# Two-layer cross-attention and FFN on one core: an own buffer for raw weight tiles, batch 0's projection and norm moved into the last two units of attention 0, and W1 loaded step by step

## The reference

```
layer 0:  q   = qdq(norm(x)) @ qdq(wq).T + bq          # qdq: int8 codes with a scale per row
          k,v = context @ wkv.T + bkv                  # 16 heads of 32
          o   = softmax(q k / sqrt(32)) v
          x   = x + qdq(o) @ qdq(wp).T + bp
          h   = layernorm(x) @ W1.T                    # W1 is 2048 x 512
          x   = x + gelu(round(h / 0.1) * 0.1) @ W2.T
layer 1:  cross-attention with a mask, output projection, norm, small FFN with experts
```

## Time and profile before

| | |
|---|---|
| median of 3 runs | 2798.19 us (2797.98 to 2801.25) |
| profiled execution | 2802.59 us, its span 2800.8 us |
| PE busy | 2595.8 us (93%), mean granted clock 0.974 |
| DVE busy | 1809.8 us (65%) |
| ACT busy | 1247.3 us (45%) |
| POOL busy | 1209.9 us (43%) |
| DMA | 400.61 MB, 143 GB/s over the span |

### The profile page before, as it was taken

One profiled execution on the slowest core, in us unless ns is written; L12 is line 12 of the kernel. 1 busy time (PEld: TensorE's weight loads), 2 busy tenths in 40 slices (PEclk: granted clock), 3 DMA queues, 4 the chain that ended last, 5 costly groups with the idle time before them and its releaser, 6 DMA issues. The chain is left out here.

```text
span 2800.8 us, 35487 instructions
## 1 busy us (share of the span) xinstructions
PE 2595.8 (93%) x14024; PEld 1676.8 (60%) x14024; DVE 1809.8 (65%) x2539; ACT 1247.3 (45%) x1873; POOL 1209.9 (43%) x302
## 2 busy tenths in 40 slices
PE   8999899998999999999967998998899999998898
PEld 7888788886444454444425777776343334334676
DVE  4553544556666676766615666554799999996664
ACT  3221212312656656565642222222687878773211
POOL 1000000002999999999950000000577777774110
PEclk9999999999999999999987999999999999998899
DMA  8576666565353534435017434435877777762100
GB/s 296 202 251 217 228 234 239 195 195 140 78 110 62 120 67 99 89 78 109 17 55 261 143 134 165 141 125 132 203 155 156 156 156 156 156 183 98 60 31 31
DMA packets 214856, 400.61 MB, mean 143 GB/s; under 512 B 16697, under 2 KB 92505, under 8 KB 214625
## 3 DMA queue, kind: packets, MB, share of 16 engines
q1 hardware_dynamic: 214688, 398.34, 51.1%
HBM read 256.31 MB, written 140.33 MB: 142 GB/s over the span
## 5 line engine op out<-in xcount | busy, mean ns | idle before, releaser
L1176 POOL TENSOR_TENSOR pooled<-pooled,probs 128x2048 f32<-128x2048 f32 x140 | 640.5, 4575 | 20.1
L1085 ACT ACTIVATE probs<-psum 128x512 f32<-128x512 f32 (+1 forms) x832 | 459.3, 598 | 354.7 <-PE psum L1011 351.7
L1112 DVE TENSOR_REDUCE win_max<-psum 128x1 f32<-128x802 f32 x480 | 453.9, 988 | 168.9 <-PE psum L976 168.7
L1886 DVE TENSOR_SCALAR probs<-psum,bound 128x1024 f32<-128x1024 f32 (+1 forms) x416 | 507.5, 1278 | 43.8 <-PE psum L1782 43.8
L1841 ACT ACTIVATE probs<-probs 128x1024 f32<-128x1024 f32 (+1 forms) x416 | 440.6, 1059 | 112.7 <-DVE probs L1886 74.9
L1917 POOL TENSOR_TENSOR pooled<-pooled,probs 128x2048 f32<-128x2048 f32 x80 | 368.4, 4605 | 79.9 <-ACT probs L1841 79.9
L1011 PE MATMUL psum<-q_st,k_st 128*128 128x512 f32 (+1 forms) x832 | 336.0, 438 | 37.1 <-ACT den_sb L1097 17.9
L1011 PEld LDWEIGHTS psum<-q_st,k_st 128*128 128x128 f32 (+1 forms) x832 | 148.9, 185 | 260.0 <-ACT probs L1085 176.3
L197 POOL TENSOR_TENSOR r_q<-ve_q,minus_half 128x4 f32<-128x4 f32 x8 | 8.7, 1087 | 681.7 <-DVE ve_q L173 681.7
L976 PE MATMUL psum<-k_st,q_st 96*128 96x402 f32 x960 | 266.3, 359 | 6.1 <-DVE o_sb L1143 5.0
L1782 PE MATMUL psum<-q_st,k_st 128*128 128x512 f32 (+1 forms) x832 | 250.8, 423 | 10.2 <-PEq L138 10.2
(11 more groups left out here) (242 smaller groups left out, 4461.8 us busy)
## 6 DMA issues: line engine op xcount, KB each, us to landing
k_st<-k_hi SPq DMA_DIRECT2D x64, 801.0 KB, 11.9
k_st<-k_lo SPq DMA_DIRECT2D x48, 801.0 KB, 11.5
k_hi<-kt_hi SPq DMA_DIRECT2D x32, 801.0 KB, 4.1
k_lo<-kt_lo SPq DMA_DIRECT2D x32, 801.0 KB, 6.2
v_rows<-v_out SPq DMA_DIRECT2D x96, 256.0 KB
v_st<-v_rows SPq DMA_DIRECT2D x24, 768.0 KB
q_st<-q_hi SPq DMA_DIRECT2D x64, 256.0 KB, 10.3
w<-w_hi_d SPq DMA_DIRECT2D x64, 256.0 KB, 3.0
```

Of the source, the lines that this page charges most:

```text
L1085: A.activation(probs[i % NPROBS][0:rows, j, :], bank(score_banks.where["score", u, t, j])[0:rows, :], ACT.Exp, scale=1.0 / ROOT).then_inc( ...
L1112: V.tensor_reduce(win_max[:, r, j, c:c + 1], window(windows.where["max", u, i])[:, :, 0:MV], AX.XY, ALU.max).then_inc(max_done, 1)
L1176: G.tensor_tensor(pooled[u % 2][:], before[:], probs[tile(u, k) % NPROBS][:], ALU.add).then_inc(pool_added, 1)
L1886: V.tensor_scalar(probs[i % NPROBS][0:rows, half * W:half * W + W, :], window(("score", u, t, half))[0:rows], bound[0:rows, u // NG, t:t + 1],
```

## The change

Three things are changed.

1. In the first stage h_raw has a place of its own. SP loads the next raw tile right behind the stores of the last job, in the same tick, without the wait for h_stored. The jobs start at tick 18 and not 12. Layer 0's eight tiles pass through v_out and h_raw, layer 1's through full and step_row two at a time with all low halves on DVE; on ACT and DVE layer 1's tiles come later, from tick 8 on. v_out has three buffers, not four.
2. The projection and norm of batch 0 move from the start of the FFN stage into attention_0. Their tiles (class FirstRows) lie in the place of slot 1, which is free after unit 13. SP loads them at the start of unit 14. DVE quantises behind the spread at tile 11 of unit 14. PE turns the codes at tile 0 of unit 15 (DVE copies them, not ACT) and multiplies at tile 2, through the PSUM windows of the maxima; DVE adds the rows at tile 2 and normalises at tile 4, and POOL takes the root ahead of its last add.
3. W1's chunks 0 to 4 are loaded at the start of the FFN stage, each later one in the step NW2 to FT - 2 of batch 0, behind the W2 chunk of that step. x of batch 1, wq and the mask are loaded in steps 5, 9, 10 and 12, and the waits for wq's semaphore move to where it is used.

The diff's core, in this order: SP's jobs, the two sets of weight tiles and SP's turns for layer 1's; in attention_0 the transposes on PE and their place, DVE's places, and POOL's root; in the FFN stage SP's loads of W1.

```
                 def halves():
-                    for j in range(len(weights.stage), len(weights.tiles)):
-                        weights.on_sp(j)
-                        yield
-                    for _ in range(FIRST_JOB - len(weights.tiles) + len(weights.stage)):
-                        yield
-                    for n, (src, hi, lo) in enumerate(halved):
-                        if n:
-                            Y.wait_ge(h_stored, 32 * n)
+                    for _ in range(FIRST_JOB):
+                        yield
+                    weights[0].wait_staged(Y)
+                    for n, (src, _, _) in enumerate(halved):
                         load(h_raw[:], src, h_landed)
-                        for _ in range(JOB_TICKS - 1):
+                        for _ in range(JOB_TICKS if n else JOB_TICKS - 1):
                             yield
                         Y.wait_ge(h_lo_done, n + 1)
-                        for dst, part in ((hi, h_hi), (lo, h_lo)):
+                        for dst, part in zip(halved[n][1:], (h_hi, h_lo)):
                             store(dst, four(part[:]) if len(dst.shape) == 3 else part[:], h_stored)
-                        yield
...
+            weights = [SplitWeights(sem, v_out + [h_raw], "wa"), SplitWeights(sem, [full, step_row], "wb", pool=False)]
...
+                    def weights_1():
+                        for _ in range(4):
+                            yield
+                        for j in range(2 * KT):
+                            if j == 2:
+                                for _ in range(7):
+                                    yield
+                            if j >= 2:
+                                yield
+                                yield
+                            weights[1].on_sp(j)
...
+                    def first_codes():
+                        for half in range(2):
+                            slot, free = windows.take(("codes", half))
+                            M.wait_ge(*free)
+                            if half == 0:
+                                M.wait_ge(o_coded, 1)
+                            for w in range(2):
+                                m = transposes(window(slot)[:, w, :], first.cols, 2 * half + w)
+                            m.then_inc(q_ps, 1)
+                            windows.freed_by(q_turned, half + 1)
...
+                            if now == (UNITS - 1, 0):
+                                first_codes()
+                            if now == (UNITS - 1, 2):
+                                first_projection()
...
+                        if now == (UNITS - 2, TURN_AT):
+                            V.wait_ge(o_landed, 16)
+                            for _ in quantise_on_dve(own, first.cols, first.step, first.recip, o_coded):
+                                pass
+                        if now == (UNITS - 1, 0):
+                            first_codes()
+                        if now == (UNITS - 1, 2):
+                            first_rows()
+                        if now == (UNITS - 1, CLOSE_AT):
+                            V.wait_ge(y_done, RT)
+                            for _ in norm_on_dve(own, nm, first.rows, first.cols, 0, normed):
+                                pass
...
+                            if u == UNITS - 1 and k == pooled_tiles(u) - 2:
+                                root_on_pool(nm, 0)
...
-                    for f in range(FT):
+                    for f in range(NW2 + 1):
                         load_w1(f)
                         if f < NW2:
                             load_w2(f)
...
+                        if NW2 <= i < FT - 1:
+                            load_w1(i + 1)
+                        if i == 5:
+                            load_x(1)
```

More of the change, by code:

```diff
@@ L65, in f32, with together @@
     return ap.bitcast(F32)
+def together(*sides):
+    while sides:
+        sides = [side for side in sides if next(side, sides) is None]
+        yield
 def three(l_hi, l_lo, r_hi, r_lo):
@@ L749, in pool_program @@
                 def pool_program():
-                    for j in range(len(weights.tiles)):
-                        weights.on_pool(j)
+                    for j in range(2 * KT):
+                        weights[0].on_pool(j)
                     for b in range(B):
@@ L835, in sp_program @@
                     load(rows[:], a["wq0"].rearrange("(r p) d -> p r d", p=P), rows_landed)
-                    for j in range(KT, len(weights.stage)):
-                        weights.on_sp(j)
-                    beside = halves()
+                    for j in range(KT, 2 * KT):
+                        weights[0].on_sp(j)
+                    beside = together(weights_1(), halves())
                     for b in range(B):
@@ L1369, in second_half @@
                             m.then_inc(f_read, 1)
-                    for _ in projected(0):
-                        pass
                     operand(0)
@@ L2288, in out_projection_and_ffn_1 @@
                 close()
+        handover = ExitStack()
+        with ExitStack() as brief:
+            first = FirstRows(allocator(brief, "right"))
+        k_1, q_1 = (allocator(handover, "right")(name, shape, F32R)
+                    for name, shape in (("k_st01", [P, HPG, TP]), ("q_st01", [P, HPG, S])))
         with ExitStack() as scope:
```

246 lines of the change are left out of this document (154 added, 92 removed).

## The result

| | before | after |
|---|---|---|
| median of 4 runs | 2798.22 us | 2757.27 us (2754.22 to 2758.67) |
| ratio, 95% interval | | 0.9847 [0.9835, 0.986] |
| profiled execution, span | 2802.59, 2800.8 us | 2758.67, 2756.8 us |
| mean granted clock | 0.974 | 0.981 |
| DVE busy | 1809.8 us | 1842.0 us |

The change makes the kernel 41 us faster by the medians and 44.0 by the two spans. In the changed kernel's lines, L168 are products (L150 before), L173 transposes (L155), L219 to L234 the quantisation (L201 to L216), L1219 the spread (L1130), L1300 POOL's additions (L1176), L1252 to L1258 batch 0's rows, L786 the value tiles (L739).

A forecast was written before the change was run, and what follows sets the result against it. PE carries the program almost everywhere and loses time standing still, worst at the handover from 1400 us, then in the first stage. −20 − 33.6 + 18.4 = −35.2 us takes the median 2798.19 to 2763, range 2746 to 2779.

The forecast's parts named there:

- rival (1): Attention 0: DVE and POOL don't hinder each other, PE waits 3.4 us instead of 8.3; 2754 us, chance 0.16.
- Own raw buffer (first stage): First stage: earlier raw-tile loads remove 16.7 us of waits, plus 6 of clock, less 3 charged; 20 us less.
- the list of waits: First stage: PE waits taken off, 5.5 us for wq, 4.9 of the 7.4, 3.2 and 3.1; 16.7 us.
- The 3 us charged for layer 1's weights and three value buffers: First stage: cost of two weight buffers with one tick of lead, low halves on DVE, and less value-buffer slack; 3 us.
- What leaves the handover: Attention 0's last matmul to the first with W1: 44.5 us become 11.0, later W1 tiles free; 33.6 us less.
- What comes into attention 0: Units 14 and 15: quantise wait 8.3 us, window wait 2.8, transposes, projection and clock; 18.4 us more.
- POOL's adds near 5.3 in unit 15: Sign in attention 0: POOL's additions in unit 15 would take near 5.3 us in the changed profile.
- (2): First stage: splitting layer 1's weights gives back the gain, 5 us instead of 20; 2778 us, chance 0.15.
- (3): Unit 15: turn taking costs about 6 to 8 us more, only 6 us of room; 2770, chance 0.13 with (5).
- (4): First stage: three value buffers make DVE wait for stores, slower; 2804 us or more, chance 0.04.
- (5): FFN stage, batch 0: W1 by step comes late, giving back perhaps 5 us; chance 0.13 with (3).

The follow-up runs named there:

- w1_at_once: Changed kernel with all sixteen W1 tiles, x of batch 1, the mask and wq loaded at the FFN stage's start, as before the change; 2778.6 us.
- pool_short: Changed kernel with POOL's additions of tiles 6 to 10 of unit 14 cut to 64 of 2048 elements, leaving out most of them; 2747.2 us.
- own_raw: Kernel before the change with h_raw in its own place, the next raw tile loaded right behind the stores, and three value buffers; 2792.8 us.
- codes_early: Changed kernel with DVE's quantisation of batch 0's rows cut into four pieces in tiles 5 to 8 of unit 14; 2754.0 us.

## Why the prediction was right

The time, 2757.3 us, lies 5.7 us below the forecast of 2763, inside its range, and by the mechanism forecast. The time alone would not have told: rival (1) stood at 2754, and the changed kernel run again gave 2754.7. It is the stretches and the waits that decide. By the spans the change gives 44.0 us against 35.2 forecast; the 8.8 us are 6.6 in the first stage, 4.0 not foreseen in the FFN stage, 0.5 in attention 0, less 0.6 at the handover and 1.7 in the two stretches for which nothing was forecast.

- **Own raw buffer (first stage), −20: the cause held, the size was 6.6 us too small.** Against my sum, the part up to the first root gave 8.5 us and not 5.5 plus a share of the clock, and the rest 18.1 us. Here the windows fit better than the list of waits: from 200 to 500 us PE's busy time rose by 13.8 us, and the clock's rise from 0.95 to 0.98 and from 0.98 to 1.00 is 5 more. The 3 us charged for layer 1's weights and three value buffers were not seen anywhere: PE is busy for 89.89 of the 90 us from 10 to 100.
- **What leaves the handover, −33.6: −33.0.** Right, but one step of it was judged wrongly. I wrote of W1's later tiles "no cost, their cover is these steps", and took the third part of the change for an edit without weight. It costs nothing, but without it 24 of the 33 us are given back (w1_at_once). Before, the 44.5 us of the projection were also the cover under which 13 MB came in; I took the projection away and did not ask what had been loaded under it, and who stood behind it in SP's queue.
- **What comes into attention 0, +18.4: +17.9.** The waits of 8.07 and 2.96 us (8.3 and 2.8), the multiplications of 5.83, the transposes at 1.2 GHz are as reckoned, and pool_short shows that taking turns is the cause. The rule of the Trainium skill's page "SBUF — State Buffer" (Who interferes with whom) that stood beside the 8.3 is borne out here on both sides: two-input additions and in-place multiplications wait for POOL's whole instruction, the reduction does not. Which of DVE's modes was at work no row names. The sign "POOL's adds near 5.3 in unit 15" did not come: they take 4.55 to 5.03 us. It was mostly DVE that waited.
- **Not foreseen, −4.0:** the FFN stage's first steps at a higher clock. I had the transposes "at 1.2 GHz as now", which they are (3.65 us), and stopped there; before, the clock was low for longer behind them (0.91 over 43 us, against 1.00). No run isolates this: in the change run again the clock was 0.97 over 43 us, worth 2.6 us, and the stretch 5.8 us shorter than before.
- **Rivals.** (1), no hindrance, falls by the 8.07. (2), the first stage gives back, falls by the windows. (3) falls, and by more than I reckoned: the root's small operation was held for 4.52 us, a thing I had not counted, but POOL's last addition ended at 1434.0, DVE was done at 1436.6 and PE at 1445.6, so there were some 9 us of room and not 6. (4), three value buffers: DVE waited 11.8 us in six places, not tens of microseconds, and own_raw, with three, was faster than the kernel before, with four. (5), W1 late by step: behind the first W1 matmul PE waits 1.2 us at most up to 1560 us.

## What to carry to other kernels

A stall that a change removes may have been cover for something: before it goes, list every transfer that was issued under it and what stands in the queue behind, or the stall comes back under another name. Where two engines exclude each other for whole instructions, even a small operation waits as long as the other's instruction lasts; moving the work earlier or later moved or lengthened the wait here, and only an interval in which the other engine was silent took most of it away. One trace of a kernel can differ from the next by several microseconds in stretches that the edit does not touch; read a small effect between marks. When a buffer is shared out anew, look at every use of it, also the short one at the start.

## What the runs showed of the hardware

DVE operations with two inputs in SBUF, and multiplications and scalings of SBUF tiles in place, waited for POOL's 4.6 us additions whatever their own size: one of 128x4 with two inputs took 4.52 us instead of 0.16, one scaling of 128x2048 took 5.40 instead of 1.23, four multiplications of 128x512 took 10.18 instead of 1.67. A reduction of 128x2048 did not wait: 2.29 us beside an addition, as alone.

Behind a stop of PE of 2.16 or 3.50 us the sixteen transposes ran at 2.4 GHz (1.94 us). Behind stops of 8.07 to 8.12 and of 9.44 us they ran at 1.2 GHz (3.62 to 3.65 us), and behind those of 6.42 to 6.52 us at the head of the FFN stage they took 3.44 to 3.65 us. The length of the stop does not decide alone: behind the wait for the window, 2.96 us in the changed kernel, four transposes took 0.66 us, and behind the same wait in codes_early they took 1.11, at a granted clock of 0.50 over the next 2 us. What made the difference no run shows.

```profile
1410.81 1.11 PE L1057 MATMUL psum<-ident,acc_sb 128*128 128x128 f32 x4 [2.97 <-DVE o_y L1252]
```
